# Denominators of two relations' sums as two leading columns of ones in the features

## The reference

```python
x = _layernorm(x + _L0_gnn_ref(x, ...), axis=-1)
x = _layernorm(x + _L1_gnn_ref(x, edge_index, edge_type_3, ...), axis=-1)
x = _layernorm(x + _L2_gnn_ref(x, edge_index, edge_type_4, ...), axis=-1)
x = _layernorm(x + _L3_gnn_ref(x, ...), axis=-1)

# _L1_gnn_ref: two of these, with elu between them; heads is 4, then 1
def rgat_conv(x, W, q, k, b, src, dst, etype, heads, out_ch, n_nodes):
    xr = jnp.einsum('nd,rdf->rnf', x, W)
    oi = xr[etype, dst]
    oj = xr[etype, src]
    alpha = jax.nn.leaky_relu(oi @ q + oj @ k, NEG_SLOPE)
    m = jax.ops.segment_max(alpha, dst, num_segments=n_nodes)
    e = jnp.exp(alpha - m[dst])
    z = jax.ops.segment_sum(e, dst, num_segments=n_nodes)
    a = e / (z[dst] + EPS)
    msg = (a[:, :, None] * oj.reshape(-1, heads, out_ch)).reshape(-1, heads * out_ch)
    return jax.ops.segment_sum(msg, dst, num_segments=n_nodes) + b
```

## Time and profile before

| | us |
|---|---|
| Median of 3 runs | 1694.26 |
| Lowest and highest run | 1692.98, 1698.70 |
| Span of the profiled execution | 1694.3 |
| PE busy in it | 1641.7 (97%) |
| VectorE busy | 1076.7 (64%) |
| ScalarE busy | 683.8 (40%) |
| GpSimd busy | 648.5 (38%) |

### The profile page before, as it was taken

One profiled execution on the slowest core, in us unless ns is written; L12 is line 12 of the kernel. 1 busy time (PEld: TensorE's weight loads), 2 busy tenths in 40 slices (PEclk: granted clock), 3 DMA queues, 4 the chain that ended last, 5 costly groups with the idle time before them and its releaser, 6 DMA issues. The chain is left out here.

```text
span 1694.3 us, 23124 instructions
## 1 busy us (share of the span) xinstructions
PE 1641.7 (97%) x8371; PEld 1416.2 (84%) x8371; DVE 1076.7 (64%) x2095; ACT 683.8 (40%) x1094; POOL 648.5 (38%) x606
## 2 busy tenths in 40 slices
PE   7999999999999999999999999899999999999998
PEld 4378799999999988789866999888888888999977
DVE  8757888787787866876798466854313321444646
ACT  4333544444344344424666443423243324332231
POOL 0042152433523323237777755314244224422421
PEclk9899999999999999999999998999999999999999
DMA  4246131321312233134000323113222222323241
GB/s 125 73 161 239 34 104 56 103 75 57 119 60 83 80 108 103 32 106 143 29 0 1 115 76 108 50 54 97 81 85 88 78 81 84 97 79 106 84 133 45
DMA packets 57177, 145.33 MB, mean 86 GB/s; under 512 B 13936, under 2 KB 17136, under 8 KB 56048
## 3 DMA queue, kind: packets, MB, share of 16 engines
q1 hardware_dynamic: 50448, 111.11, 21.3%
q10 hardware_dynamic: 6624, 32.77, 5.5%
HBM read 131.80 MB, written 12.06 MB: 85 GB/s over the span
## 5 line engine op out<-in xcount | busy, mean ns | idle before, releaser
L913 POOL TENSOR_TENSOR w_pair<-early,w_pair 128x384 fp32r<-128x384 f32 x468 | 489.8, 1084 | 879.8 <-ACT w_pair L1685 879.8
L997 PE MATMUL ps<-w_pair,cols_x 128*128 128x384 f32 x2088 | 377.0, 337 | 1.8 <-POOL w_pair L913 1.2
L997 PEld LDWEIGHTS ps<-w_pair,cols_x 128*128 128x128 f32 x2088 | 362.1, 188 | 7.7 <-issue 3.4
L997 PE MATMUL ps<-w_pair,wide 128*128 128x384 f32 x1728 | 303.0, 335 | 0.3 <-DVE early L2117 0.3
L1685 ACT ACTIVATE w_pair<-early 128x768 fp32r<-128x768 f32 x234 | 182.4, 839 | 298.5 <-PE ps L997 130.0
L997 PEld LDWEIGHTS ps<-w_pair,wide 128*128 128x128 f32 x1728 | 299.5, 188 | 3.5 <-issue 2.5
L1622 PE MATMUL ps<-wide,w_pair 128*128 128x512 f32 x972 | 227.7, 392 | 3.4 <-DVE wide L2114 3.4
L1622 PEld LDWEIGHTS ps<-wide,w_pair 128*128 128x128 f32 x972 | 181.0, 188 | 43.9 <-DVE wide L2114 5.8
L1135 PE MATMUL ps<-prob,wide 128*128 128x512 f32 x576 | 137.5, 399 | 0.2 <-DVE yt L2216 0.2
L1570 PE MATMUL ps<-prob,wide 128*128 128x512 f32 x546 | 137.0, 390 | 0.0
L1135 PEld LDWEIGHTS ps<-prob,wide 128*128 128x128 f32 x576 | 109.1, 190 | 26.9 <-issue 4.0
(11 more groups left out here) (332 smaller groups left out, 2170.1 us busy)
## 6 DMA issues: line engine op xcount, KB each, us to landing
early<-weights SPq DMA_DIRECT2D x246, 384.0 KB, 3.1
edge_mask<-counts ACTq DMA_DIRECT2D x13, 512.0 KB, 3.2
multi<-attn ACTq DMA_DIRECT2D x8, 768.0 KB, 4.3
kept<-early ACTq DMA_DIRECT2D x3, 1536.0 KB, 6.1
counts<-tally SPq DMA_DIRECT2D x12, 256.0 KB, 4.5
multi<-kept ACTq DMA_DIRECT2D x2, 1536.0 KB, 6.5
edge_mask<-masks ACTq DMA_DIRECT2D x5, 512.0 KB, 3.4
last_raw<-weights SPq DMA_DIRECT2D x6, 384.0 KB, 5.6
```

Source lines behind the costliest of these rows:

```text
L913: return nc.gpsimd.tensor_tensor(dst, whole, high.bitcast(F32), ALU.subtract)
L997: mm = nc.tensor.matmul(ps[:, m, 0:HW], left[:, a, k, m * P:(m + 1) * P], w_pair[:, slot_of[0], b, k, :], start=(k == 0 and a + b == 0), s ...
```

## The change

For relations 0 and 1 of this convolution, each source block's features get two columns ahead of them, ones in the high part and zeros in the low one. The first half of the features is then one matmul of 386 columns in place of 384, and the first column of its PSUM bank is the denominator. The separate two-column matmuls of these two relations go. The buffers `wide0` and `wide1` grow by 16 elements a partition; `led[r]` is the view with the ones and `rows_last[r]` the view of the features behind them. The features thus start two elements (8 bytes) later in every block of 770, and the second half starts at element 386.

GpSimd writes the ones and zeros (`lead_with_ones`) when relation 0's first tile has been copied, with a semaphore `ones_led` that PE waits for. VectorE reads the denominator of each target block from column 0 of its bank, one element a partition, right ahead of the features of that bank, copied in relation 0 and added in relation 1. Relation 2 is as before and so is the four-head convolution ahead. Counts of `misc_done` move by two, and PE no longer waits for `den_read` ahead of relations 1 and 2.

```diff
+ONES = 2 * NB * 2
-        wide = [sb("wide0", [P, 2, KB * N], F32R)]
+        wide = [sb("wide0", [P, 2 * KB * N + ONES], F32R)]
...
+        led = [wide[i][:].rearrange("p (a m f) -> p a m f", a=2, m=NB) for i in range(2)]
+        rows_last = [led[0][:, :, :, 2:], led[1][:, :, :, 2:], rows[2]]
...
+            def lead_with_ones():
+                for r in range(2):
+                    for a, value in enumerate((1.0, 0.0)):
+                        nc.gpsimd.memset(led[r][:, a, :, 0:2].bitcast(F32), value).then_inc(ones_led, 1)
...
                         pool.wait_ge(tile_copied, first_tile + 8 * r + u + 1)
-                        low_of(rows[r][:, 1, m, part], hv[:, m % 2], rows[r][:, 0, m, part]).then_inc(rows_low, 1)
+                        if target is rows_last and (r, u) == (0, 0):
+                            lead_with_ones()
+                        low_of(target[r][:, 1, m, part], hv[:, m % 2], target[r][:, 0, m, part]).then_inc(rows_low, 1)
...
                 for s in range(NB):
                     pe.wait_ge(x_lo, x_base + s + 1)
                     for m in range(NB):
-                        for a in range(2):
-                            mm = nc.tensor.matmul(ps[:, 5, 2 * m:2 * m + 2], weights_of[:, a, s, m * P:(m + 1) * P], ones[:, 0:2],
-                                                  start=(s + m + a == 0), stop=(s + a == NB), skip_group_check=True)
-                    if s == NB - 1:
-                        mm.then_inc(misc_done, 1)
-                    for m in range(NB):
...
-                            mm = nc.tensor.matmul(ps[:, (units - 8 + m) % RING, 0:HW], weights_of[:, a, s, m * P:(m + 1) * P], source[:, b, s, 0:HW],
+                            mm = nc.tensor.matmul(ps[:, (units - 8 + m) % RING, 0:HW + 2], weights_of[:, a, s, m * P:(m + 1) * P],
+                                                  source[:, b, s, 0:HW + 2],
                                                   start=(s + a + b == 0), stop=(s == NB - 1 and a == 1), skip_group_check=True)
...
-                                                  source[:, b, s, HW:D],
+                                                  source[:, b, s, HW + 2:],
...
             pe.wait_ge(rows_low, 32)
-            row_sums(rows[0], prob_sets[0], 140, tile_copied, 109, 8, {2: last_source}, dotted=85, late=spread_last_source)
-            pe.wait_ge(den_read, 2)
+            pe.wait_ge(ones_led, 4)
+            row_sums(led[0], prob_sets[0], 140, tile_copied, 109, 8, {2: last_source}, dotted=85, late=spread_last_source)
             pe.wait_ge(rows_low, 40)
-            row_sums(rows[1], prob_sets[1], 144, row_read, 12, 16, {1: turn_last_uv, 2: spread_last_uv})
-            pe.wait_ge(den_read, 3)
+            row_sums(led[1], prob_sets[1], 144, row_read, 12, 16, {1: turn_last_uv, 2: spread_last_uv})
...
-                    bank = ps[:, (8 * r + u) % RING, 0:HW]
+                    at = 2 * (1 - n)
+                    bank = ps[:, (8 * r + u) % RING, at:at + HW]
                     dve.wait_ge(row_done, 8 + 8 * r + u + 1)
+                    if n == 0:
+                        total, found = zc[:, 0, m:m + 1], ps[:, (8 * r + u) % RING, 0:1]
+                        ins = copy(total, found) if r == 0 else add(total, total, found)
+                        ins.then_inc(den_read, 1) if m == NB - 1 else mark(ins)
...
-            read_denominators(79, True)
             read_rows(0, range(NB))
...
-            read_denominators(83, False)
             dve.wait_ge(row_read, 16)
+            dve.wait_ge(den_read, 2)
             read_rows(1, range(NB))
```

More of the change, by code:

```diff
@@ L151, in count_and_weigh @@
         front = 2 * KB * N * 4 * 2
-        sb("unused", [P, (front - 2 * CHUNKS * P * 2 - SMALL_BYTES) // 4], F32)
+        sb("unused", [P, (front - 2 * CHUNKS * P * 2 - SMALL_BYTES) // 4 + ONES], F32)
         with nc.sbuf_tensor("slot_hot", [P, CH, P], F16) as slot_hot:
@@ L658, in graph_layers @@
             pass
-        wide = [sb("wide0", [P, 2, KB * N], F32R)]
+        wide = [sb("wide0", [P, 2 * KB * N + ONES], F32R)]
         with nc.sbuf_tensor("first_resid", [P, 2, KB * N], F32) as first_resid:
             pass
-        wide += [sb("wide1", [P, 2, KB * N], F32R)]
+        wide += [sb("wide1", [P, 2 * KB * N + ONES], F32R)]
         with nc.sbuf_tensor("mask_rows", [P, REL3, NB, N], BF16) as mask_rows:
             pass
-        wide += [sb("wide2", [P, 2, KB * N], F32R)]
+        wide += [sb("wide2", [P, 2 * KB * N], F32R)]
         with nc.sbuf_tensor("fourth_parts", [P, 4, NB, N], I16) as fourth_parts:
@@ L708, in graph_layers @@
         q_rows = alpha[0:4, :]
-        rows = [wide[i][:].rearrange("p a (m f) -> p a m f", m=NB) for i in range(3)]
+        rows = [wide[i][:, 0:2 * KB * N].rearrange("p (a m f) -> p a m f", a=2, m=NB) for i in range(3)]
+        led = [wide[i][:].rearrange("p (a m f) -> p a m f", a=2, m=NB) for i in range(2)]
+        rows_last = [led[0][:, :, :, 2:], led[1][:, :, :, 2:], rows[2]]
         resid1 = second_resid[:, 0, :].rearrange("p (m f) -> p m f", m=NB)
@@ L713, in graph_layers @@
         b_row0 = first_resid[:, 1, 0:D]
-        cols_y = [wide[i][:].rearrange("p a (k n) -> p a k n", k=KB) for i in (2, 1)]
+        cols_y = [wide[i][:, 0:2 * KB * N].rearrange("p (a k n) -> p a k n", a=2, k=KB) for i in (2, 1)]
         prob_sets = [prob, cols_x]
@@ L734, in graph_layers @@
         wt_cols = [r_den[:], multi[:, 2560:2560 + N]]
-        wk_row = wide[2][0:8, :, 0:D]
+        wk_row = wide[2][0:8, 0:2 * D].rearrange("p (a f) -> p a f", a=2)
         hv_rows = hv.rearrange("p a n -> p (a n)")
@@ L805, in graph_layers @@
         wkq_ready = sem("wkq_ready")
+        ones_led = sem("ones_led")
         p_used = sem("p_used")
@@ L933, in probability_low, with relation_low @@
                 low_of(prob_sets[r % 2][:, 1, s, :], y_ring[t % 3], prob_sets[r % 2][:, 0, s, :]).then_inc(x_lo, 1)
-            def relation_low(first_tile, first_pass, ahead=None):
+            def lead_with_ones():
+                for r in range(2):
+                    for a, value in enumerate((1.0, 0.0)):
+                        nc.gpsimd.memset(led[r][:, a, :, 0:2].bitcast(F32), value).then_inc(ones_led, 1)
+            def relation_low(first_tile, first_pass, target, ahead=None):
                 for r in range(REL3):
@@ L951, in _ @@
                     weights_low(slot, i * 6 + 3 * slot)
-            relation_low(64, 34)
+            relation_low(64, 34, rows)
             items = relational_items()
@@ L967, in _ @@
                     low_of(cols_x[part, 1, f, :], y_ring1[i % 3][part], cols_x[part, 0, f, :]).then_inc(x_lo, 1)
-            relation_low(88, 40, ahead=lambda: probability_low(0))
+            relation_low(88, 40, rows_last, ahead=lambda: probability_low(0))
             for t in range(1, REL3 * NB):
@@ L1952, in _ @@
                         high(140, y_ring[0], prob_sets[0][:, 0, 0, :])
-                    copy_tile(38 + 2 * r + n, m, n, 88 + 8 * r + u, rows[r], first=True, lows=24 + 8 * r + u)
+                    copy_tile(38 + 2 * r + n, m, n, 88 + 8 * r + u, rows_last[r], first=True, lows=24 + 8 * r + u)
                     if m == 3 and 2 * r + n < 5:
@@ L1977, in _ @@
             act.dma_start(resid1, kept).then_inc(res_in, 16)
-            copy_rows(81, 4)
-            copy_uv(82, uv_sets2[0])
+            copy_rows(80, 4)
+            copy_uv(81, uv_sets2[0])
             exponentials(2)
@@ L2072, in _ @@
                     finish_columns(layer, j + 8, j + 10, True)
-            act.wait_ge(misc_done, 89)
+            act.wait_ge(misc_done, 87)
             nc.scalar.activation(v_bc[:], ps[:, 6, :], ACT.Sqrt)
@@ L2675, in _ @@
             probabilities(1)
-            read_denominators(79, True)
             read_rows(0, range(NB))
             dve.wait_ge(mask_in, 16 * 6)
-            relation_logits(2, 80, 24, 148)
+            relation_logits(2, 79, 24, 148)
             read_rows(0, range(NB, 8))
@@ L2694, in _ @@
             wait_steps()
-            read_denominators(84, False)
+            read_denominators(82, False)
             invert_denominators(4)
@@ L2743, in _ @@
                     if layer == 0:
-                        dve.wait_ge(misc_done, 84 + r + 1)
+                        dve.wait_ge(misc_done, 82 + r + 1)
                         nc.vector.transpose(scale_bc[:, r], ps[:, 5, :]).then_inc(deg_read, 1)
```

## The result

| | before | after |
|---|---|---|
| Median (lowest to highest), 15 runs each, us | 1694.06 (1691.46 to 1702.01) | 1702.25 (1699.26 to 1707.11) |
| Span of the profiled execution, us | 1694.3 | 1701.5 |

What follows compares the result with a forecast made beforehand. PE, busy 97% of the span, was taken to bound the kernel up to the end of relation 1's first half, then VectorE's chain. 1694.3 - 4.0 - 3.4 + 0.1 + 0.4 = 1687.4 us, range 1685.0 to 1691.5.

Steps and rivals of the forecast that it cites:

- Added: List of the edit's new costs in relations 0 and 1: 0.1 us on PE and 0.4 us on VectorE counted.
- two columns: Two more columns on 96 matmuls of relations 0 and 1 at 0.48 ns a column: 0.1 us.
- the reads 8 bytes off: All 192 matmuls of relations 0 and 1 read rows starting 8 bytes later: taken as nothing, bound 35 us.
- four adds: VectorE's one-element denominator adds in relation 1, 0.07 to 0.16 us each, taken as 0.1: 0.4 us in all.
- four memsets: GpSimd's four memsets ahead of relation 0's low halves: 0.5 us in all, expected to cost the kernel nothing.
- Rival 3: Shifted rows read more slowly in 192 matmuls of relations 0 and 1: 1722 or mildly 1690.9 us; 8% slower, 3% mild.
- Removed: Eight groups of eight two-column matmuls in relations 0 and 1: 3.86 + 3.4 = 7.3 us on the path.
- L1015's wait: Relation 0: PE waits for ScalarE's alpha from 1030.8 to about 1032.65; L1015 starts 4.0 us earlier than before.
- the 3.4 us: Relation 1's four two-column groups, 0.80 to 0.92 us each, removed: its first half gets 3.4 us shorter.
- The clock: Relation 0: without the two-column groups, the half-speed stretch near 1020 lasts 3.4 us and not 10.3.
- rival 1: Relation 0's clock gives nothing (1688.7), or, second form, falls again after the new idle time (1689.1); 25% together.
- Rival 2: A wait takes the place: ScalarE's copy or uvc, each under 1 us in hand, comes late; 1689.5 us, 13%.

Runs made afterwards that it cites:

- e1: Kernel before with two unused 64-byte gaps behind wide0 and wide1, giving the addresses of after, no instruction changed: 1705.48 us, ratio 1.0061.
- e2: Kernel before with a small 64-byte buffer moved between wide1 and wide2, shifting wide2, prob and w_pair: 1701.54 us, one run.
- e3: Kernel before with 256 bytes of small buffers moved between wide1 and wide2: 1696.73 us, one run.
- e6: Kernel before with 64-byte gaps and two small buffers moved behind wide0 and wide1, 256 bytes each, without the edit: 1696.96 us, ratio 1.0022.
- e4: Kernel before with 512 bytes of small buffers moved between wide1 and wide2: 1692.86 us, one run.
- e7: Kernel before with one unused 128-byte gap ahead of all the large buffers, so all move alike: 1694.78 us, one run.
- e9: Kernel before with a small 128-byte buffer moved between wide1 and wide2: 1704.15 us, one run.
- e10: Kernel before with a small 192-byte buffer moved between wide1 and wide2: 1703.36 us, one run.
- e11: Kernel before with a small 32-byte buffer moved between wide1 and wide2: 1707.89 us, one run.
- e12: e8 with ScalarE's copy of alpha put ahead of the last exponentials of relation 1: 1686.52 us, ratio 0.9965 to before.
- e5: After with a 192-byte buffer behind each of wide0 and wide1, filling the growth up to 256 bytes: 1690.74 us, ratio 0.9983 to before.
- e8: e5 with GpSimd's low halves of the last weights pass held back until relation 2's factors are done: 1688.55 us, ratio 0.9982 to before.

## Why the prediction was wrong, point by point

**The step that failed** is the list headed *Added*. It prices two columns, the reads 8 bytes off, four adds and four memsets, and it ends at the place of the change. It has no term for the 16 elements by which `wide0` and `wide1` grow, though front and diff both show the growth. That term is +11.5 us (e1 against before; 15.7 us of work at full speed in their profiles), more than the whole forecast gain, and it falls on some 4900 matmuls from 104 us on to the end. No rival had it. Rival 3 came nearest, with an operand off its place, but it looked at 192 matmuls and at the 8 bytes within the buffer; the buffers behind it were the thing to look at.

**Removed, 7.3 us; and L1015's wait, 4.0 us saved up to there.** The wait was forecast as 1.85 us and is 1.77, for ScalarE's alpha. What it gives is less than I said. PE is released at 1036.99 - 1019.40 = 17.6 us after the place's start in after and 1036.80 - 1019.17 = 17.6 in e1, which has the groups: in relation 0 VectorE's probabilities and the copy behind them set the end, with or without the groups. The 4.0 of the forecast was the comparison with an execution in which the clock was low for 10.3 us. That execution was also longer than most: in the runs listed with both, the span is 1.7 to 2.9 us below the time, mostly 1.9, so a span of 1694.3 belongs to a time of about 1696.2 (an estimate), and that it equals the median of 1694.26 is chance. In relation 1 the 3.4 us are there: 13.2 us from its start to the second half in e1 (1043.66 to 1056.86), 11.1 in after (1045.41 to 1056.47), of which 1.15 are a new wait.

**The clock.** That it is low for 3.4 us near 1020 is right; that the two-column groups held it low for 10.3 is not shown. Windows of after, as in the earlier trace rows:

```profile
1024.00:1030.00 6.00, 5.44 (x22) 5.44 (x23) 4.14 (x5) 3.39 (x7) 3.02 (x3) 0.72 0.00 1
1037.00:1045.00 8.00, 8.00 (x35) 7.75 (x36) 6.19 (x17) 0.85 (x1) 7.57 (x9) 0.79 0.31 94
```

6 x 0.28 x 2 = 3.4 us. But kernels that keep the groups had about 10 (before, e2, e3, e6), 3.4 (e4, e7) and none (e1, e9, e10, e11) there. One profile of before could not tell a cause from a case. The second row is rival 1 in its second form: behind the new idle time of 1.77 the clock falls again, 8 x 0.21 x 2 = 3.4 us, and the 36 matmuls of the second half take 8.0 us against 6.4 in e1 and e12. It did so in e5 too. In e8, with an idle time of 1.76 at the same place, it did not fall.

**Rival 2, a wait takes the place,** came true beside the forecast: 0.7 us of slack in `uvc` became a wait of 1.15. I took VectorE's chain at the duration it has in before; from the first of its small operations to the last it takes 4.8 us (1046.08 to 1050.91) and took 3.0 in before (1044.09 to 1047.06), 1.9 more, because more of them fell beside GpSimd's. That is the 0.7 and the 1.15 together.

**Added.** The 386-column matmuls have the normal rate (2.18 us for 12 in relation 0, 2.21 in relation 1), so rival 3's place is not slower to speak of: 173.3 ns became 174.4 in e5 for L1306 over 48 matmuls, which is 0.2 us over 192. VectorE's four adds (rows of the relation 1 sums of after):

```profile
1055.19 0.15 DVE L2123 TENSOR_TENSOR zc<-zc,ps 128x1 f32<-128x1 f32 x1 [4.28 <-PE ps L1295]
1055.26 0.55 DVE L2123 TENSOR_TENSOR early<-early,ps 128x384 f32<-128x384 f32 x1
1055.72 0.15 DVE L2123 TENSOR_TENSOR zc<-zc,ps 128x1 f32<-128x1 f32 x1
```

Each shows 0.15 us but puts the next off by only 0.07, so four cost 0.3 and not 0.4. The 0.126 of the Trainium skill ("VectorE: DVE Perf Modes", the TRN2 errata) lies between the two. The four memsets take 0.2 us instead of 0.5.

**The sum, mended.** e5 and e6 differ by the edit alone, 6.2 us by medians; e1 and after by 3.2, with a new low stretch and a full 1.15 us wait. The forecast edit was 6.9. With the missing term, 1687.4 + 11.5 = 1698.9; the rest to after's 1702.25 is what the edit brings less than I said. By the profiled executions: addresses +15.7, edit -6.2, idle time +3.6, clock -5.9 make +7.2, from 1694.3 to 1701.5.

**Open.** What in the chip makes the distance of the operands count; why e6 has the low clock in more of its executions than before; and when the clock falls near 1020.

## What to carry to other kernels

A buffer that grows moves all that lie behind it: before pricing such an edit, list the addresses of the big matmul operands before and after, and give the growth back with a filler so that stationary and moving operand keep their distance (here modulo 256 bytes). When the span moves and the place doesn't, compare the period of equal runs of matmuls far from the place, start to start over the count. And a term that is read off one low-clock stretch of one execution is a range and not a value: compare the granted clock of the profiled execution with that of the other runs first.

## What the runs showed of the hardware that was not expected

For the fp32 matmuls of this kernel, the period of a matmul with its weight load depends on how far apart its two operands lie in the state buffer. At full clock 512 columns take 232.4 ns at a distance of 0, 256 or 512 bytes (modulo 2048, from before's layout), and 234.6, 238.1, 238.9 and 238.9 at 64, 128, 192 and 32. 384 columns take 174.6 and up to 177.2. Moved alike, both operands by 128, 512 columns stay at 232.4. For one kernel this is 0.7% of its time and hides a whole optimisation. The Trainium skill, "TensorE: Matmul & The Clock Gate", section "Step-by-step: what each phase is for", has the two operands read through ports of their own, so that loading weights takes nothing from the running matmul. By that the distance would not matter; the measurement decides, and here it does by up to 6.5 ns in 232.
